# VectorE's maxima head by head around the copy of a turned head, and one scaling of the maxima, in a two-layer attention kernel on one core

## Chip, cores and metric

One core of one Trainium2 chip runs the whole kernel. The metric is the device time in microseconds, the median of the runs. TensorE is called PE in the profile, VectorE DVE, ScalarE ACT, GpSimd POOL; PEld is TensorE's loading of weights, which overlaps its products.

## The reference, cut to what matters

32 batches of x (112 rows of 256) and of a context (375 rows of 256) go through two layers. Each layer has a cross attention with 16 heads and a feed-forward part. What the change touches is the softmax of both attentions:

```python
# layer 0, 16 heads of width 64
sim = einsum('bihd,bjhd->bhij', q, k) * DIM_HEAD ** -0.5
attn = softmax(sim, axis=-1)              # over 375 positions
# layer 1, 16 heads of width 16, q and k normalised per head, then rotated
q = rms_norm(q, q_norm_w); k = rms_norm(k, k_norm_w)
attn = softmax(einsum('bhtd,bhsd->bhts', rope(q), rope(k)) * D ** -0.5, axis=-1)
```

The softmax subtracts the maximum of each row. In layer 1 the kernel multiplies q's normalising factor (one number for each row and head, in `qrs`) not into q, but into the exponential as its scale; so the negated maximum has to be multiplied by the same factor.

## The kernel before, in words

Everything of a batch lives on chip. Each engine runs its own instruction list, written out by hand, and they meet at semaphores. After an opening part (layer 0 of batch 0) each engine runs a loop of 31 batches: `rest(b)`, which finishes layer 0 and the first feed-forward part and already projects keys, values and queries of batch b+1, and `attention(MIDDLE, b)`; a closing part does layer 1 of the last batch, and the second feed-forward part of all batches follows.

The attention goes by pairs of heads. The MIDDLE part has 16 pairs, i = 0 to 15: pairs 0 to 3 and 12 to 15 are of layer 0 (of the next batch), pairs 4 to 11 of layer 1. At step i the engines do the following, in this order:

- TensorE: `scores(i+2)` (L409, two heads, into two of the four banks of `ps`), `turn(i-1)` (L419, three transposes for each head of the pair, into the two banks of `pt`), and at odd steps from 3 the products with the values, `values0` (L431) or `values1` (L446), for earlier pairs. At the last two steps come projections of keys and values.
- VectorE: `row_max(i+2)`, `row_sum(i+1)` (L1024, the reciprocal of the sums), `turned(i-1)` (L999, the copy of the odd head's transposes from `pt` into `probT`).
- ScalarE: its own `turned(i-1)` (L734, the copy of the even head), then `exps(i+2)` (L773, two exponentials, each with its sum read out by a second instruction).
- GpSimd: the product of pair i+1 with the reciprocals (L1442), and in the first steps four roots for `qrs`.

The waits that tie them together:

- `scores(j+2)` waits for `exped`, the exponentials of pair j, since `ps` holds two pairs.
- `row_max(j)` waits for `scores(j)` of both heads; `exps(j)` waits for `maxed`.
- `turned(i-1)` waits for `pT`, the turn of its head.
- the second head of `turn(i)` waits for `pT_odd`, VectorE's copy of the turn before; the first head for `pT_even`, ScalarE's.
- `row_sum(i+1)` waits for the exponentials of pair i+1.

For layer 1, `row_max` before is a reduction, a wait of VectorE on itself (`link`, a semaphore `dve_steps`), at even pairs a wait for GpSimd's root (`q1_rstd`), and two scalings (L1016), one for each head. `HEADS1` puts heads h and h+4 together as a pair.

Of the kernel before, what the change touches and what calls it, by code (L numbers as in the profile page):

```python
# [10 lines left out]
ALU = mybir.AluOpType  # L11
ACT = mybir.ActivationFunctionType
AX_X = mybir.AxisListType.X
# [8 lines left out]
U8_EPS = 1e-8  # L22


DVE_STEPS = 29
POOL_STEPS = 7


# [24 lines left out]
def xattn_ffn_kernel(nc, A, x3_dram, out):  # L53
    B, T, D = A["x"].shape
    S = A["ctx"].shape[1]
    INNER = A["wq0"].shape[1]
    F = A["f0w1T"].shape[1]
    H = 16
# [16 lines left out]
    PAIRS = H // 2  # L75
    HEADS1 = [8 * c + n for c in range(DC) for n in (0, 4, 2, 6, 1, 5, 3, 7)]

    with ExitStack() as ctx:
        def sb(name, shape, dt=F32):
            return ctx.enter_context(nc.sbuf_tensor(name, shape, dt))  # L80

        def sem(name):
            return ctx.enter_context(nc.semaphore(name))


        ps = ctx.enter_context(nc.psum_tensor("ps", [P, 4, 512], F32))
# [86 lines left out]
        qrs = sb("qrs", [T, 3, H])  # L173
# [3 lines left out]
        nmx = sb("nmx", [T, 2 * H])  # L177
# [7 lines left out]
        def flat(t, dt=F32):  # L185
# [24 lines left out]
            "const_in wk0_in wv0_in wkv1_in f0w1_in f0w2_in late_in w_hi w_lo ident_ready zeros_ready "  # L210
            "wsum_ready wsum_done w_quant f1w1_in f1w2_in "
            "x_in ctx_in cT_ready cT_hi cT_lo k0_ready k0_sb v0_ready v0_sb var0 rstd0 xn0_ready xT0_ready xT0_sb "
            "q0_ready q0_sb xbo_ready scores maxed exped recip normed pT pT_even pT_odd pv o_sb wo_ready x1_ready "
            "var1 rstd1 xq_ready diag_ready xqT_ready rb_ready xqT_sb rb_sb kv1_ready kv1_sb h_ready h_sb conv0 "
            "conv_ready tanh_ready y_ready yT_ready am_ready hr_ready hq_ready hqT_ready hqT_sb ffn_ready x2_ready "
# [5 lines left out]
        s = {n: sem(n) for n in names}  # L221
        block = ctx.enter_context(nc.Block())

        AHEAD = 2
# [5 lines left out]
        OPENING, MIDDLE, CLOSING = range(3)  # L230

        def pair_of(i, part):

            if part == OPENING:
                return 0, i
            if part == CLOSING:
                return 1, i
            if i < LEAD:
                return 0, i
            return (1, i - LEAD) if i < LEAD + PAIRS else (0, i - PAIRS)  # L240

        def at(i, part, b):

            return i if part == OPENING else b * G + (PAIRS + i)
# [718 lines left out]
        def _(dve):  # L963
            step = Steps(s["dve_steps"], DVE_STEPS)

            def link(ins):
                step.link(dve, ins)
# [28 lines left out]
            def turned(i, part, b):  # L996

                dve.wait_ge(s["pT"], 2 * at(i, part, b) + 2)
                dve.tensor_copy(probT[:, 2 * (i % 4) + 1, :, :],  # L999
                                pt[0:SK, 1, 0:KT * T].rearrange("p (k t) -> p k t", k=KT))\  # L1000
                    .then_inc(s["pT_odd"], 1)

            def row_max(i, part, b):

                layer, p = pair_of(i, part)
                g = layer * H + 2 * p
                dve.wait_ge(s["scores"], at(i + 1, part, b))
                top = dve.tensor_reduce(nmx[:, g:g + 2], ps[0:T, 2 * (i % 2):2 * (i % 2) + 2, 0:S], AX_X, ALU.max,  # L1008
                                        negate=True)
                if layer == 1:  # L1010
                    link(top)
                    if p % 2 == 0:
                        dve.wait_ge(s["q1_rstd"], b * 4 + (p // 2 + 1))
                    for n in range(2):
                        h = HEADS1[2 * p + n]
                        top = dve.tensor_scalar(nmx[:, g + n:g + n + 1], nmx[:, g + n:g + n + 1], qrs[:, 2, h:h + 1],  # L1016
                                                None, ALU.mult)
                top.then_inc(s["maxed"], 1)

            def row_sum(i, part, b):  # L1020
                layer, p = pair_of(i, part)
                g = layer * H + 2 * p
                dve.wait_ge(s["exped"], at(i + 1, part, b))
                dve.reciprocal(rinv[:, g:g + 2], rsum[:, g:g + 2]).then_inc(s["recip"], 1)  # L1024

            def query_masks(b):
                dve.wait_ge(s["q1T_ready"], b + 1)
                dve.tensor_tensor(q1[:, 0, :, :], pt[:, 0, 0:T].unsqueeze(1).to_broadcast([P, 4, T]),
                                  mask1[:].unsqueeze(2).to_broadcast([P, 4, T]), ALU.mult).then_inc(s["q1_sb"], 1)

            def query_squares(b):
                dve.wait_ge(s["q1_sq"], b + 1)
                link(dve.tensor_reduce(qrs[:, 0, :], qsq.rearrange("p (h e) -> p h e", e=DH1), AX_X, ALU.add))
                dve.tensor_scalar(qrs[:, 1, :], qrs[:, 0, :], 1.0 / DH1, RMS_EPS, ALU.mult, ALU.add)\
                    .then_inc(s["q1_var"], 1)
# [51 lines left out]
            def attention(part, b):  # L1087
                count = G if part == MIDDLE else PAIRS
                k = 0 if part == OPENING else b + 1
                for i in range(count):  # L1090
                    if part == OPENING and i in (2, 4, 6):
                        ternary(1, i // 2 + 1)
                    if i + AHEAD < count:
                        row_max(i + AHEAD, part, b)
                    if part == MIDDLE and i == 0:
                        query_masks(b)
                    if i + 1 < count:
                        row_sum(i + 1, part, b)
                    if part == MIDDLE and i == 0:
                        query_squares(b)  # L1100
                    if i >= 1:
                        turned(i - 1, part, b)
                if part != CLOSING:
                    k1_squares(k, 0)
                    k1_squares(k, 1)
                turned(count - 1, part, b)
                if part != CLOSING:
                    k1_squares(k, 2)
                    dve.wait_ge(s["k1_sq"], k * KT + KT)
                    dve.tensor_scalar(krs[:, 1, :], krs[:, 0, :], 1.0 / DH1, RMS_EPS, ALU.mult, ALU.add)\  # L1110
                        .then_inc(s["k1_var"], 1)
                if part == MIDDLE:
                    for n in range(5):
                        x3_step(n, b)
# [17 lines left out]
            def rest(b, last_batch):  # L1132
# [76 lines left out]
                if not last_batch:  # L1209
                    q0_copy(b + 1, 1)  # L1210
                    row_max(0, MIDDLE, b)
                else:
                    scales(1, 1)
# [10 lines left out]
                if not last_batch:  # L1224
                    row_sum(0, MIDDLE, b)
                    row_max(1, MIDDLE, b)
                else:
                    query_masks(b)
                    query_squares(b)
                    for i in range(AHEAD):  # L1230
                        row_max(i, CLOSING, b)
                    row_sum(0, CLOSING, b)


# [28 lines left out]
            for rope, w in ((ropq[:].unsqueeze(1), nwq), (ropk[:], nwk)):  # L1263
                n, k = rope.shape[0], rope.shape[1]
# [327 lines left out]
```

## Time and profile before

| | |
|---|---|
| median of 3 runs | 2452.87 us (2451.51 to 2453.61) |
| profiled execution, its own time | 2455.66 us |
| its span, first to last instruction | 2453.8 us |
| TensorE busy | 2380.4 us, 97% |
| VectorE, ScalarE, GpSimd busy | 1700.6, 1584.0, 1596.3 us (69, 65, 65%) |
| one batch of the loop | 70.93 us |
| mean granted TensorE clock | 0.985 |

The profile is of one execution, so its sums are compared with its own time. A busy share is an average over the span; the timeline and the chain of waits, read in one batch, show who waits for whom. Instructions on one engine overlap a little: one starts before the record of the one ahead ends.

### The profile page before, as it was taken

What the parts mean: (1) busy time and instruction counts of PE and PEld (TensorE: products, weight loads), DVE (VectorE), ACT (ScalarE), POOL (GpSimd) and SP (SyncE); (2) the same over time, 40 slices, a digit from 0 to 9 for tenths busy, and PEclk for the clock granted to TensorE, in tenths of its full rate; (3) what the DMA queues carried; (4) which work ended last, traced back from release to release, by engine and by line L of the source; (5) the groups of instructions that cost most, each with busy time, mean ns of one, the idle gap of its engine ahead of it and who ended that gap; (6) DMA issues with size and microseconds to landing.
All of it is one profiled execution on the core that took longest, in us unless ns stands there. A gap on an engine that the chain in (4) does not pass through costs nothing.

```text
span 2453.8 us, 59494 instructions
## 1 busy us (share of the span) xinstructions
PE 2380.4 (97%) x18926; PEld 1796.5 (73%) x18926; DVE 1700.6 (69%) x4476; ACT 1584.0 (65%) x4337; POOL 1596.3 (65%) x1862
## 2 busy tenths in 40 slices
PE   7999999999999999999999999999999999999578
PEld 5777777777777777777777777777777777777336
DVE  6666666776667667666767776666677666767775
ACT  4666666766666676666666766666676666667346
POOL 2666776666667666666776666677666666766507
PEclk9999999999999999999999999999999999999689
DMA  4100000000000000000000000000000000000202
GB/s 151 35 10 10 10 8 4 8 10 10 10 10 8 10 2 10 10 10 10 10 8 4 8 10 10 10 10 8 7 5 10 10 10 10 8 4 0 55 10 61
DMA packets 34652, 37.02 MB, mean 15 GB/s; under 512 B 2932, under 2 KB 33092, under 8 KB 34628
## 3 DMA queue, kind: packets, MB, share of 16 engines
q1 hardware_dynamic: 34628, 36.71, 5.0%
q8 instruction: 14, 0.23, 0.0%
q14 instruction: 10, 0.08, 0.0%
HBM read 29.36 MB, written 7.34 MB: 15 GB/s over the span
## 4 chain that ended last, share of the span: by engine, by line
PE 86%; ACT 5%; DVE 4%; issue 2%; POOL 1%; DMA 0%; ACTq 0%; POOLq 0%; DVEq 0%; SPq 0%
PE ps L334 24%; PE ps L409 15%; PE pt L419 14%; PE pa L431 5%; PE pa L466 5%; PE ps L393 5%; PE pa L446 4%; ACT prob L773 3%; PE pa L334 2%; PE pt L334 2%; PE pa L593 1%; PE pa L553 1%; DVE nmx L1008 1%; PE pt L577 1%; PE ps L459 1%
## 5 line engine op out<-in xcount | busy, mean ns | idle before, releaser
L1008 DVE TENSOR_REDUCE nmx<-ps 112x2 f32<-112x750 f32 x512 | 476.5, 936 | 203.4 <-PE ps L409 203.3
L1442 POOL TENSOR_TENSOR prob<-prob,rinv 112x375 f32<-112x375 f32 x512 | 404.0, 810 | 286.6 <-DVE rinv L1024 280.6
L1442 POOL TENSOR_TENSOR f1w_room<-f1w_room,rinv 112x375 f32<-112x375 f32 x512 | 404.6, 814 | 33.4 <-DVE rinv L1024 27.2
L734 ACT ACTIVATE room<-ps 128x375 f32<-128x375 f32 (+2 forms) x480 | 227.8, 488 | 278.3 <-PE ps L334 278.3
L999 DVE COPY probT<-pt 125x336 f32<-125x336 f32 x512 | 253.0, 494 | 98.8 <-PE pt L419 98.6
L734 ACT ACTIVATE probT<-pt 125x336 f32<-125x336 f32 x512 | 233.7, 456 | 107.8 <-PE pt L419 104.9
L419 PEld LDWEIGHTS pt<-ident,prob 112*125 112x125 f32 x1536 | 191.5, 189 | 130.3 <-issue 91.7
L419 PEld LDWEIGHTS pt<-ident,f1w_room 112*125 112x125 f32 x1536 | 197.8, 188 | 119.4 <-POOL f1w_room L1442 52.7
L1465 POOL TENSOR_TENSOR krs<-krs,nhalf 125x48 f32<-125x48 f32 x32 | 256.9, 8028 | 0.0
L419 PE MATMUL pt<-ident,f1w_room 112*125 112x112 f32 x1536 | 238.2, 287 | 2.8 <-DVE probT L999 1.2
L419 PE MATMUL pt<-ident,prob 112*125 112x112 f32 x1536 | 239.1, 291 | 0.0
L409 PE MATMUL ps<-kT,q 64*112 64x375 f32 x1024 | 231.3, 530 | 5.8 <-ACT prob L773 1.6
L409 PE MATMUL ps<-room,q 64*112 64x375 f32 x1024 | 220.5, 518 | 3.0 <-ACT prob L773 1.9
L773 ACT ACTIVATE prob<-ps,nmx 112x375 f32<-112x375 f32 x256 | 144.4, 569 | 84.8 <-DVE nmx L1008 83.2
L773 ACT ACTIVATE prob<-ps,nmx,qrs 112x375 f32<-112x375 f32 x256 | 169.0, 674 | 45.3 <-DVE nmx L1016 45.3
L773 ACT ACTIVATE f1w_room<-ps,nmx,qrs 112x375 f32<-112x375 f32 x256 | 168.3, 668 | 33.3 <-DVE nmx L1016 33.3
L431 PE MATMUL pa<-probT,room 125*64 125x112 f32 x3072 | 183.6, 265 | 0.0
L1429 POOL TENSOR_TENSOR st<-st,lneps 112x1 f32<-112x1 f32 x96 | 18.2, 190 | 252.6 <-DVE st L990 252.6
L431 PEld LDWEIGHTS pa<-probT,room 125*64 125x64 f32 x3072 | 149.2, 137 | 24.9 <-issue 11.0
L773 ACT ACTIVATE f1w_room<-ps,nmx 112x375 f32<-112x375 f32 x256 | 144.3, 571 | 4.6 <-DVE nmx L1008 1.4
L334 PE MATMUL ps<-cT_hi,wk_lo 128*128 128x376 f32 x512 | 138.2, 351 | 6.7 <-DVE cT_lo L972 6.7
L1169 DVE SCALAR_TENSOR_TENSOR z<-hp,convw,z 128x112 f32<-128x112 f32 x512 | 138.7, 330 | 3.5
(262 smaller groups left out, 5168.7 us busy)
## 6 DMA issues: line engine op xcount, KB each, us to landing
ctok<-in_ctx SPq DMA_DIRECT2D x32, 375.0 KB
xin<-in_x SPq DMA_DIRECT2D x32, 112.0 KB, 2.0
x_rows<-x SPq DMA_DIRECT2D x32, 112.0 KB, 1.9
out<-probT SPq DMA_DIRECT2D x16, 224.0 KB, 2.3
room<-x_rows SPq DMA_DIRECT2D x1, 2576.0 KB, 13.9
stage<-in_f1w SPq DMA_DIRECT2D x2, 1024.0 KB, 5.3
stage<-in_wk SPq DMA_DIRECT2D x1, 1024.0 KB, 8.0
stage<-in_wv SPq DMA_DIRECT2D x1, 1024.0 KB, 10.5
```

The source lines that it names most:

```text
L334: last = pe.matmul(dst, left(l, c), right(r, c), start=(n == 0), stop=(n == len(TERMS) - 1))
L393: last = pe.matmul(ps[:, g + 1, j * T:(j + 1) * T], wq0[:, c, (HT * g + j) * P:(HT * g + j + 1) * P], xn0T[:, c, :], start=(c == 0), stop= ...
L409: last = pe.matmul(ps[0:T, 2 * (i % 2) + n, 0:S], q, k, start=True, stop=True)
L419: last = pe.transpose(pt[0:SK, n, t * T:(t + 1) * T], prob(i, n)[:, t * SK:(t + 1) * SK], ident[0:T, 0:T])
L431: last = pe.matmul(pa[r:r + DH0, p // HT, (p % HT) * T:(p % HT + 1) * T], v0[0:SK, t, h * DH0:(h + 1) * DH0], probT[:, 2 * (i % 4) + n, t, :],
L734: return act.activation(dst, src, ACT.Copy)
L773: ins = act.activation(prob(i, n), ps[0:T, 2 * (i % 2) + n, 0:S], ACT.Exp, bias=nmx[:, g:g + 1], scale=scale, accum_out=rsum[:, g:g + 1])
L999: dve.tensor_copy(probT[:, 2 * (i % 4) + 1, :, :], pt[0:SK, 1, 0:KT * T].rearrange("p (k t) -> p k t", k=KT))\
L1008: top = dve.tensor_reduce(nmx[:, g:g + 2], ps[0:T, 2 * (i % 2):2 * (i % 2) + 2, 0:S], AX_X, ALU.max, negate=True)
L1169: ins = dve.scalar_tensor_tensor(z[:, j, :], hp[:, j, tap:tap + T], convw[:, j, tap:tap + 1], z[:, j, :], ALU.mult, ALU.add)
L1442: pool.tensor_tensor(prob(i, n), prob(i, n), rinv[:, g:g + 1].to_broadcast([T, S]), ALU.mult).then_inc(s["normed"], 1)
L1465: step.link(pool, pool.tensor_tensor(krs[:, 2, :], krs[:, 1, :], nhalf[0:SK, :], ALU.pow))
```

## The change

In every even step from 2 on that still has a pair i+2 to come, VectorE takes the maximum of the first head of pair i+2, then copies the odd turned head of pair i-1, then takes the maximum of the second head. In the other steps the maximum is taken over both heads at once, as before, and the copy stays last. The scaling of the maxima in layer 1 leaves `row_max`: it becomes `max_scale`, one tensor-tensor operation for both heads, which stands behind `row_sum(i+1)` and waits for a new semaphore `top1` that the last reduction raises, in place of VectorE's wait on itself (so a batch has 21 of these linked steps and not 29).

```diff
-DVE_STEPS = 29
+DVE_STEPS = 21
@@
-            def row_max(i, part, b):
+            def row_max(i, part, b, heads=slice(0, 2)):
 
                 layer, p = pair_of(i, part)
-                g = layer * H + 2 * p
+                g, m = layer * H + 2 * p, 2 * (i % 2)
                 dve.wait_ge(s["scores"], at(i + 1, part, b))
-                top = dve.tensor_reduce(nmx[:, g:g + 2], ps[0:T, 2 * (i % 2):2 * (i % 2) + 2, 0:S], AX_X, ALU.max,
-                                        negate=True)
+                top = dve.tensor_reduce(nmx[:, g + heads.start:g + heads.stop],
+                                        ps[0:T, m + heads.start:m + heads.stop, 0:S], AX_X, ALU.max, negate=True)
+                if heads.stop == 2 and layer == 0:
+                    top.then_inc(s["maxed"], 1)
+                elif heads.stop == 2:
+                    top.then_inc(s["top1"], 1)
+
+            def max_scale(i, part, b):
+                layer, p = pair_of(i, part)
                 if layer == 1:
-                    link(top)
+                    g, h = H + 2 * p, HEADS1[2 * p]
+                    assert HEADS1[2 * p + 1] == h + 4
+                    dve.wait_ge(s["top1"], b * PAIRS + (p + 1))
                     if p % 2 == 0:
                         dve.wait_ge(s["q1_rstd"], b * 4 + (p // 2 + 1))
-                    for n in range(2):
-                        h = HEADS1[2 * p + n]
-                        top = dve.tensor_scalar(nmx[:, g + n:g + n + 1], nmx[:, g + n:g + n + 1], qrs[:, 2, h:h + 1],
-                                                None, ALU.mult)
-                top.then_inc(s["maxed"], 1)
+                    dve.tensor_tensor(nmx[:, g:g + 2], nmx[:, g:g + 2], qrs[:, 2, h:h + 5:4], ALU.mult)\
+                        .then_inc(s["maxed"], 1)
@@ in attention, for each i
-                    if i + AHEAD < count:
+                    between = i >= 2 and i % 2 == 0 and i + AHEAD < count
+                    if between:
+                        row_max(i + AHEAD, part, b, slice(0, 1))
+                        turned(i - 1, part, b)
+                        row_max(i + AHEAD, part, b, slice(1, 2))
+                    elif i + AHEAD < count:
                         row_max(i + AHEAD, part, b)
                     if part == MIDDLE and i == 0:
                         query_masks(b)
                     if i + 1 < count:
                         row_sum(i + 1, part, b)
+                    if i + AHEAD < count:
+                        max_scale(i + AHEAD, part, b)
                     if part == MIDDLE and i == 0:
                         query_squares(b)
-                    if i >= 1:
+                    if i >= 1 and not between:
                         turned(i - 1, part, b)
@@ in rest, last batch
                     for i in range(AHEAD):
                         row_max(i, CLOSING, b)
+                        max_scale(i, CLOSING, b)
```

## Rows read from the trace of the kernel before

**Rows 1.** The page: busy us, share of the span, instructions of each engine.

```profile
PE 2380.4 (97%) x18926; PEld 1796.5 (73%) x18926; DVE 1700.6 (69%) x4476; ACT 1584.0 (65%) x4337; POOL 1596.3 (65%) x1862
```

**Rows 2.** Windows, one batch: length, each engine's busy time, granted clock, DMA.

```profile
1023.73:1094.66 70.93, 70.78 (x573) 53.84 (x574) 49.44 (x135) 47.08 (x132) 48.16 (x58) 1.00 0.03 9
```

**Rows 3.** Timeline of steps 8 and 9: start, length, engine, line, idle time before.

```profile
1040.93 0.89 PE L409 MATMUL ps<-kT,q 64*112 64x375 f32 x4
...
1041.75 0.91 PE L419 MATMUL pt<-ident,f1w_room 112*125 112x112 f32 x6
1041.87 0.94 DVE L1008 TENSOR_REDUCE nmx<-ps 112x2 f32<-112x750 f32 x1 [0.54 <-PE ps L409]
...
1042.93 0.33 DVE L1016 TENSOR_SCALAR nmx<-nmx,qrs 112x1 f32<-112x1 f32 x2
...
1043.26 0.49 DVE L999 COPY probT<-pt 125x336 f32<-125x336 f32 x1
...
1043.40 1.03 PE L419 MATMUL pt<-ident,prob 112*125 112x112 f32 x6
...
1043.43 0.67 ACT L773 ACTIVATE f1w_room<-ps,nmx,qrs 112x375 f32<-112x375 f32 x1 [0.62 <-DVE nmx L1016]
1043.66 0.93 DVE L1008 TENSOR_REDUCE nmx<-ps 112x2 f32<-112x750 f32 x1
...
1044.64 0.20 ACT L773 ACTIVATION_READ_ACCUMULATOR f1w_room<-ps,nmx,qrs 112x1 f32 x1
...
1045.08 0.89 PE L409 MATMUL ps<-room,q 64*112 64x375 f32 x4
```

**Rows 4.** Chain that ended last, steps 2 to 5: start, length, what.

```profile
1028.07 0.95 DVE nmx L1008
...
1029.25 0.35 DVE nmx L1016 x2
...
1033.52 0.26 ACT prob L773
...
1033.82 0.89 PE ps L409 x4
```

**Rows 5.** Timeline of TensorE alone, steps 3 to 6.

```profile
1029.60 1.16 PE L419 MATMUL pt<-ident,f1w_room 112*125 112x112 f32 x6
...
1032.81 0.91 PE L419 MATMUL pt<-ident,f1w_room 112*125 112x112 f32 x6
...
1036.78 0.57 PE L409 MATMUL ps<-kT,q 64*112 64x375 f32 x2
```

**Rows 6.** VectorE's groups by form: out<-in, count, busy us, mean ns, idle.

```profile
L1184 DVE TENSOR_REDUCE am<-pa 112x1 f32<-112x512 f32 x64 | 43.9, 686 | 4.2 <-PE pa L553 0.5
...
L1039 DVE TENSOR_REDUCE krs<-room 125x16 f32<-125x256 f32 x96 | 39.9, 416 | 111.9 <-ACT v L734 111.9
...
L972 DVE TENSOR_TENSOR cT_lo<-ps,cT_hi 128x375 fp32r<-128x375 f32 x64 | 32.1, 544 | 18.3 <-ACT cT_hi L734 18.3
...
L1322 DVE TENSOR_TENSOR t<-t 128x2 f32<-128x2 f32 x1 | 0.2, 161 | 0.0
```

**Rows 7.** Timeline of steps 12 to 14.

```profile
1049.10 0.89 PE L409 MATMUL ps<-room,q 64*112 64x375 f32 x4
...
1050.04 0.94 DVE L1008 TENSOR_REDUCE nmx<-ps 112x2 f32<-112x750 f32 x1 [0.95 <-PE ps L409]
...
1051.01 0.57 ACT L773 ACTIVATE f1w_room<-ps,nmx 112x375 f32<-112x375 f32 x1
...
1052.03 0.20 ACT L773 ACTIVATION_READ_ACCUMULATOR f1w_room<-ps,nmx 112x1 f32 x1
...
1052.19 0.45 ACT L734 ACTIVATE probT<-pt 125x336 f32<-125x336 f32 x1
...
1053.12 0.58 PE L419 MATMUL pt<-ident,prob 112*125 112x112 f32 x3
```

**Rows 8.** Windows, 40 us behind the loop, in the closing part.

```profile
2280.00:2320.00 40.00, 22.28 (x92) 14.14 (x94) 28.39 (x73) 15.75 (x42) 23.91 (x16) 0.50 0.16 39
```

More of the change, by code:

```diff
@@ L212, in xattn_ffn_kernel @@
             "x_in ctx_in cT_ready cT_hi cT_lo k0_ready k0_sb v0_ready v0_sb var0 rstd0 xn0_ready xT0_ready xT0_sb "
-            "q0_ready q0_sb xbo_ready scores maxed exped recip normed pT pT_even pT_odd pv o_sb wo_ready x1_ready "
+            "q0_ready q0_sb xbo_ready scores top1 maxed exped recip normed pT pT_even pT_odd pv o_sb wo_ready x1_ready "
             "var1 rstd1 xq_ready diag_ready xqT_ready rb_ready xqT_sb rb_sb kv1_ready kv1_sb h_ready h_sb conv0 "
```

## The prediction

> **What bounds the kernel now.** I read the profile from coarse to fine. The page's busy line first: TensorE is busy 97% of the span, the other three engines 65 to 69% [rows 1]. The windows of one batch say it more sharply: a batch of the steady loop takes 70.93 us and TensorE works in 70.78 us of them [rows 2]; 31 such batches are 2199 us, nine tenths of the span. The granted clock there is 1.00, the level of 2.4 GHz. So nothing that only frees VectorE (49.44 us of 70.93) can gain; the change matters where VectorE stands between two pieces of TensorE's work, in the attention.
>
> There one loop sets the pace. PSUM holds the scores of two pairs of heads, so scores(j+2) waits until ScalarE has taken the exponentials of pair j, these wait for the maxima of pair j (VectorE, "maxed"), and these wait for scores(j). Read it off for j = 10 in the timeline [rows 3], S being the start of scores(10), 1040.93. The reduction starts at 1041.87 (S+0.94) and takes 0.94; the two scalings start 0.12 after its end, at 1042.93, and take 0.33; ScalarE starts 0.17 later, at 1043.43, and its last piece ends at 1044.84, 1.41 later; TensorE starts 0.05 behind such an end (1033.78 to 1033.82 in the chain of waits [rows 4]). Sum: 0.94+0.94+0.12+0.33+0.17+1.41+0.05 = 3.96 us. TensorE comes to scores(12) at 1045.08, S+4.15. **The loop has 0.19 us of slack**, and no more.
>
> TensorE's 4.15 is not all work. The turn in step 8 (1041.75) lasts 0.91, that in step 9 (1043.40) lasts 1.03 [rows 3]: its second head waits for VectorE's copy of the turn before, which ends only at 1043.75, since VectorE has first taken the maxima and their scaling. That 0.12 recurs in step 7. In step 3 the same wait makes the turn 1.16 long, 0.25 too much [rows 5]. And scores(7) waits for ScalarE until 1033.82 [rows 4], where the turn in front, begun at 1032.81 [rows 5], ends at 1033.72 and would have given way 0.07 earlier, as scores(10) does to its turn (1041.75 against 1041.82 [rows 3]): at 1033.65, so 0.17 are lost. All that VectorE's order costs TensorE: 0.12+0.12+0.25+0.17 = 0.66 us a batch.
>
> **The change, part by part.** In the even steps 2, 4, ..., 12 (pairs 4, 6, ..., 14) the reduction over 112x750 becomes two over 112x375, with the copy of the turned odd head between them.
>
> *The copy.* It can't start before the turn of that step has ended, and TensorE does that turn behind the scores: it ends at 1041.75+0.91 = 1042.66, S+1.73. With the 0.05 that VectorE shows behind TensorE (1041.82 to 1041.87) the copy starts at S+1.78 where it started at S+2.33. It comes 0.55 earlier and takes away the three turn waits: at most 0.49 us a batch.
>
> *The second head's maximum.* It now stands behind that copy. Head 0 needs S+0.94 to S+1.49 and then VectorE idles 0.29 us for the turn. Copy to S+2.27 (0.49). The next instruction starts 0.09 before a copy's end (1043.75 against 1043.66 [rows 3]): S+2.18. Its length isn't in the trace. The nearest rows: 256 elements 416 ns, 512 elements 686 ns, and an operation over 375 elements out of PSUM 544 ns [rows 6]. Reductions thus cost about 1.05 ns an element and 150 ns for themselves; I take 0.55 us, with 0.42 and 0.69 as ends. End at S+2.73, where the whole maximum ended at S+1.88.
>
> The Trainium skill says that such a fixed cost is paid by every instruction, so that many small tiles pay it often (VectorE: DVE Perf Modes, "The TRN2 errata"); the rows above agree. Its table gives a Vector operation out of PSUM 120 cycles and one for each element, at 0.96 GHz 516 ns for 375, an estimate from that page; by it the loss below would be some 5 us smaller in all.
>
> *The scaling (layer 1).* One tensor-tensor operation over 112x2 for two tensor-scalars. A tensor-tensor over 128x2 takes 161 ns [rows 6], two scalings 0.33: 0.17 saved. The wait for the root of the same step stays, so does the 0.12 in front. Start S+2.85, end S+3.01. Ends: 0.15 and 0.21 (one of today's scalings, 0.33 for two that overlap by 0.08).
>
> *The order.* The scaling also moves behind the row sum's reciprocal, which waits for the exponentials of pair i+1. In odd steps these end about when they are needed: the maxima of pair j+1 then reach ScalarE about 0.2 us late. In even steps the row sum comes about 0.5 us later for GpSimd, which works 48.16 us of 70.93 [rows 2] and has its result needed a step later. I cost both at nothing, because the loop over the even pairs, below, is longer than either; were it not, the first would cost up to 0.19 in each of four steps.
>
> **The new loop:** 3.01 + 0.17 + 1.41 + 0.05 = **4.64 us** for layer 1, against 4.15 now and 4.03 of pure TensorE work. Without a scaling and with the shorter exponentials of layer 0 (1051.01 to 1052.23, 1.22 [rows 7]) and with ScalarE 0.03 behind a maximum (1050.98 to 1051.01 [rows 7]; no root is waited for) it is 2.73 + 0.03 + 1.22 + 0.05 = 4.03, against 4.02.
>
> Along one batch:
> - Pair 4. Maximum in front at 1028.07, so S = 1027.13. Here 0.23 lie between reduction and scaling (1029.02 to 1029.25 [rows 4]). New end of scaling: S+2.73+0.23+0.16 = 1030.25, against 1029.60: 0.65 late. From there to scores(7) the chain is ScalarE alone without a wait [rows 4], so scores(7) comes 0.65 later. That swallows the 0.25 and the 0.17.
> - Pair 6: scores(8) comes 2.96 behind scores(7) (1036.78 against 1033.82 [rows 4, 5]), and its loop, begun at scores(6), ends earlier: nothing added.
> - Pairs 8 and 10: 4.64 for 4.15, twice 0.49. The 0.12 of each is inside.
> - Pair 12: 4.03 for 4.02: 0.01.
> - Pair 14: nothing waits for its scores, but the turn of pair 13 needs ScalarE's even copy of pair 12, which is queued behind the exponentials of pair 14. These end at S+2.73+0.03+1.22 = S+3.98; the copy takes 0.45, overlapping by 0.04 (1052.19 against 1052.23), and I give TensorE 0.1 behind a copy, twice what it shows behind an exponential, for the stretched turn of 1043.40 ends 0.68 behind its copy: S+4.49. Today it starts at 1053.12, S+4.02 [rows 7]: 0.47.
>
> Sum: 0.65+0.49+0.49+0.01+0.47 = 2.11, say **2.1 us a batch**. Nothing later in the batch gives it back, since TensorE has no idle time there. 31 x 2.1 = 65.1. The opening and the closing part have two such steps each; partly at half clock, where TensorE's own work hides more, I take 0.8 together. The profiled execution took 2455.66 (span 2453.80, 1.86 outside it), so 2521.6 for it; the median of the runs lies 2.8 lower: **2519 us**, 2.7% slower. With the ends for the half maximum (0.13 either way, in four or five places) the batch loses 1.6 to 2.8 us: 2503 to 2540.
>
> **Rivals.**
> - *The copy frees TensorE (faster).* If the second head's maximum did not lie on the loop, 0.66 us a batch would come back: 20 us, 2433. It decides at a loop of 4.03 us: the half maximum and the scaling would have to end 0.6 us earlier than I find, yet the copy can't precede the turn, which ends at S+1.73. 3 in 100. That loss and gain just meet (2453): 2 in 100.
> - *Only the steady pairs pay.* ScalarE might start pair 4 later without passing it on, and the even copy of pair 12 might slip in earlier; then 2 x 0.49 remain, 31 us: 2484. Against it speaks that ScalarE runs strictly in order in [rows 4]. 12 in 100.
> - *The odd steps pay too.* The scaling behind the row sum adds 0.19 in four steps: 24 us more, 2543. For it: the wait is real. Against it: it runs beside the longer loop. 7 in 100.
> - *The clock falls.* Late in the span, where TensorE works 22.28 of 40 us, the granted clock is 0.50, its level of 1.2 GHz [rows 8]. The new loop still works 4.03 of 4.64 us, and 0.6 us is the longest hole. If it did fall in the attention, 4.03 would be 8.06 a pair of steps, 3.4 more, eight times a batch: over 800 us. The Trainium skill has the clock fall after idle time (TensorE: Matmul & The Clock Gate, "The HAM clock gate"); whether it does after holes this short no row shows. 2 in 100.
>
> My case keeps 74 in 100, with a range of its own of 2503 to 2540. The range for 8 in 10 reaches some way towards the case where only the steady pairs pay and stops at my own upper end: 2492 to 2540. About 0.2% (5 us) is what a measurement of this kernel can tell from no change: faster 0.03, same 0.02, slower 0.95.
>
> **What would show it.** In the new trace a batch takes 73.0 us, and most of the 2.1 more is TensorE idle; scores(8), (10), (12) start 4.64 apart; idle time of the weight loads in front of the scores is put down to ScalarE's exponentials, and ScalarE's to VectorE's scaling; half maxima take 0.55, one waits 0.3 for TensorE's turn between them; turns are 0.91 long, none stretched. I am wrong if the steps 8 to 11 still take 4.15 a pair, if the half maximum is far from 0.55, or if the turn, not the scores, is what waits.

## The result, and the profile after

The changed kernel takes 2516.27 us (median of 4 runs, 2514.64 to 2519.22); the kernel before takes 2452.19 beside it (2450.04 to 2453.61). The ratio is 1.0262 [1.0248, 1.0276]: 64 us slower, where 66 (2519 us) was predicted. The profiled execution took 2515.62 us, its span is 2513.8, its mean granted clock 0.987.

The page's busy line, its chain of waits in shares, and the windows of one batch, as [rows 1] and [rows 2]:

```profile
PE 2373.5 (94%) x18926; PEld 1783.7 (71%) x18926; DVE 1704.7 (68%) x4410; ACT 1571.9 (63%) x4337; POOL 1593.9 (63%) x1862
...
PE 54%; POOL 27%; issue 13%; DVE 5%; ACT 1%; DMA 0%; POOLq 0%; SPq 0%; ACTq 0%; DVEq 0%
```

```profile
1048.40:1121.37 72.97, 70.70 (x574) 53.53 (x573) 49.59 (x133) 46.70 (x132) 48.09 (x58) 1.00 0.03 8
```

A batch takes 72.97 us, 2.04 more than in [rows 2], with the same work in it (70.70 busy against 70.78) at the same clock. All of the loss is TensorE waiting, 2.27 us a batch where it was 0.15. (A turn that is stretched by a wait counts as busy for its whole length, so busy time is a little more than work.) 31 x 2.04 = 63 us.

Where it waits: steps 8 and 9 from the timeline, beside [rows 3] (S, the start of scores(10), is 1066.70).

```profile
1066.70 0.89 PE L409 MATMUL ps<-kT,q 64*112 64x375 f32 x4 [0.54 <-ACT prob L773]
...
1067.52 0.91 PE L419 MATMUL pt<-ident,f1w_room 112*125 112x112 f32 x6
...
1067.64 0.55 DVE L1008 TENSOR_REDUCE nmx<-ps 112x1 f32<-112x375 f32 x1 [0.32 <-PE ps L409]
...
1068.46 0.51 DVE L999 COPY probT<-pt 125x336 f32<-125x336 f32 x1 [0.28 <-PE pt L419]
1068.89 0.54 DVE L1008 TENSOR_REDUCE nmx<-ps 112x1 f32<-112x375 f32 x1
...
1069.21 0.91 PE L419 MATMUL pt<-ident,prob 112*125 112x112 f32 x6
...
1069.55 0.16 DVE L1023 TENSOR_TENSOR nmx<-nmx,qrs 112x2 f32<-112x2 f32 x1
...
1069.88 0.67 ACT L773 ACTIVATE f1w_room<-ps,nmx,qrs 112x375 f32<-112x375 f32 x1 [1.20 <-PE pt L419]
...
1071.08 0.20 ACT L773 ACTIVATION_READ_ACCUMULATOR f1w_room<-ps,nmx,qrs 112x1 f32 x1
...
1071.34 0.57 PE L409 MATMUL ps<-room,q 64*112 64x375 f32 x2 [0.51 <-ACT f1w_room L773]
```

The first half maximum ends at S+1.49, VectorE idles 0.28 until the turn has ended, the copy starts at S+1.76, the second half at S+2.19, the scaling at S+2.85, ScalarE at S+3.18, and the next scores at S+4.64. Where the rows of before had 0.12 stretches in the turns, both turns here are 0.91 long.

Two labels mislead. ScalarE's wait at 1069.88 is put down to a turn of TensorE; but ScalarE starts 0.17 behind the scaling's end (1069.71), as in [rows 3], and in the experiments the loop grows by just what the scaling grows. And the chain of waits runs through GpSimd, 27% of the span:

```profile
1066.92 1.58 POOL prob L1456 x2
1068.51 1.04 issue
...
1069.58 1.58 POOL prob L1456 x2
```

Between its products lie "issue" gaps, 1.04 us here and up to 1.31 in this batch. In them GpSimd waits for VectorE's reciprocal of the row sums, which stands behind the late second half: an effect, unless GpSimd's product is what TensorE waits for. An experiment below asks that.

### The profile page after: what moved, and what is told of

Its sections match the earlier page's. It is cut to its first block, busy times and chain, and to the rows that moved or that the text cites. A ratio compares the mean times of both kernels' runs of the same rounds, so it can differ in the third digit from the quotient of the medians.

```text
span 2513.8 us, 59180 instructions
## 1 busy us (share of the span) xinstructions
PE 2373.5 (94%) x18926; PEld 1783.7 (71%) x18926; DVE 1704.7 (68%) x4410; ACT 1571.9 (63%) x4337; POOL 1593.9 (63%) x1862
## 4 chain that ended last, share of the span: by engine, by line
PE 54%; POOL 27%; issue 13%; DVE 5%; ACT 1%; DMA 0%; POOLq 0%; SPq 0%; ACTq 0%; DVEq 0%
PE ps L334 23%; POOL prob L1456 13%; POOL f1w_room L1456 11%; PE pa L466 5%; PE ps L393 5%; PE pa L431 3%; PE pt L419 3%; PE ps L409 3%; POOL qrs L1499 2%; PE pt L334 2%; PE pa L593 1%; PE pa L553 1%; DVE nmx L1008 1%; PE pt L577 1%; PE ps L459 1%
## 5 line engine op out<-in xcount | busy, mean ns | idle before, releaser
L1008 DVE TENSOR_REDUCE nmx<-ps 112x2 f32<-112x750 f32 x702 | 503.7, 722 | 96.9 <-PE ps L409 96.5
L419 PEld LDWEIGHTS pt<-ident,f1w_room 112*125 112x125 f32 x1536 | 189.5, 188 | 133.8 <-POOL f1w_room L1456 69.0
L419 PE MATMUL pt<-ident,prob 112*125 112x112 f32 x1536 | 234.0, 289 | 12.2 <-POOL prob L1456 11.5
L419 PE MATMUL pt<-ident,f1w_room 112*125 112x112 f32 x1536 | 227.2, 284 | 18.5 <-ACT probT L734 16.9
L1030 DVE RECIPROCAL rinv<-rsum 112x2 f32<-112x2 f32 x512 | 82.6, 161 | 142.1 <-ACT f1w_room L773 83.5
```

Source lines behind the costliest of these rows:

```text
L419: last = pe.transpose(pt[0:SK, n, t * T:(t + 1) * T], prob(i, n)[:, t * SK:(t + 1) * SK], ident[0:T, 0:T])
L1008: top = dve.tensor_reduce(nmx[:, g + heads.start:g + heads.stop], ps[0:T, m + heads.start:m + heads.stop, 0:S], AX_X, ALU.max, negate=True)
```

## The experiments

Each edit is made to the changed kernel. "Two scalings" stands for this edit of `max_scale`, the two operations of the kernel before in place of the one:

```diff
-                    dve.tensor_tensor(nmx[:, g:g + 2], nmx[:, g:g + 2], qrs[:, 2, h:h + 5:4], ALU.mult)\
-                        .then_inc(s["maxed"], 1)
+                    for n in range(2):
+                        h = HEADS1[2 * p + n]
+                        top = dve.tensor_scalar(nmx[:, g + n:g + n + 1], nmx[:, g + n:g + n + 1], qrs[:, 2, h:h + 1],
+                                                None, ALU.mult)
+                    top.then_inc(s["maxed"], 1)
```

All are read by the starts of TensorE's scores in one batch near the middle of the loop, in us:

| kernel | batch | scores 4 to 7 | 7 to 8 | 8 to 10 | 10 to 12 | 12 to 14 | median us | ratio |
|---|---|---|---|---|---|---|---|---|
| before | 70.93 | 6.69 | 2.96 | 4.15 | 4.15 | 4.02 | 2452.2 | 1 |
| after | 72.97 | 7.25 | 2.96 | 4.63 | 4.64 | 4.06 | 2516.3 | 1.0262 |
| scale_only | 71.07 | 6.92 | 3.13 | 4.02 | 4.02 | 4.02 | 2455.9 | 1.0024 [1.0014, 1.0034] |
| split_only | 71.08 | 6.92 | 3.12 | 4.03 | 4.03 | 4.02 | 2453.1 | 1.0011 [1.0001, 1.0020] |
| order_only | 73.48 | 7.43 | 2.96 | 4.81 | 4.81 | 4.03 | 2532.8 | 1.0337 [1.0320, 1.0354] |
| sum_in_hole | 73.97 | 7.25 | 2.95 | 5.13 | 5.12 | 4.06 | 2545.3 | 1.0392 [1.0375, 1.0409] |
| two_behind | 70.87 | 6.69 | 2.95 | 4.09 | 4.11 | 4.08 | 2450.3 | 0.9997 [0.9988, 1.0007] |
| hole_two | 74.24 | 7.43 | 3.13 | 5.00 | 4.99 | 4.24 | 2556.7 | 1.0438 [1.0422, 1.0455] |
| head_two | 70.72 | 6.42 | 3.13 | 4.02 | 4.02 | 4.03 | 2442.9 | 0.9968 [0.9956, 0.9980] |
| once_two | 70.73 | 6.61 | 2.96 | 4.08 | 4.09 | 4.02 | 2445.8 | 0.9981 [0.9972, 0.9991] |
| order_2 | 71.66 | 7.43 | 2.95 | 4.15 | 4.15 | 4.03 | 2474.1 | 1.0100 [1.0083, 1.0117] |
| order_6_8 | 72.13 | 6.61 | 2.96 | 4.80 | 4.81 | 4.02 | 2489.3 | 1.0158 [1.0141, 1.0175] |
| order_12 | 71.33 | 6.61 | 2.96 | 4.15 | 4.15 | 4.02 | 2464.7 | 1.0061 [1.0044, 1.0078] |
| hole_at_once | 73.64 | 7.43 | 3.13 | 4.81 | 4.81 | 4.03 | 2535.8 | 1.0349 [1.0331, 1.0366] |

The ratio of each is to runs of the kernel before beside it, whose medians were 2451.0 us for the first four experiments and 2449.5 and 2450.3 for the next two groups of four.

### Which part of the change costs the time

**scale_only**: no copy between; the whole maximum, the one scaling still behind the row sum.

```diff
-                    between = i >= 2 and i % 2 == 0 and i + AHEAD < count
+                    between = False
```

> Only the scaling is changed (one operation, behind the row sum); the maxima stay whole and the copy last. Theory (the loss is the loop through the late second maximum): with that maximum back in front, the loop is 0.17 us shorter than in the kernel before, the copy ends 0.25 earlier, and the four small waits of TensorE (0.66 us a batch) go: a batch of 70.27 us, about 2432 us. Rival 'the scaling behind the row sum's wait costs the time': slower than 2452, near 2500. Rival 'split or order costs nothing, GpSimd's late row sum is the bound': here the row sum comes no later than before, so 2452 or a little less.

**split_only**: two half maxima without the copy between them.

```diff
                         row_max(i + AHEAD, part, b, slice(0, 1))
-                        turned(i - 1, part, b)
                         row_max(i + AHEAD, part, b, slice(1, 2))
@@
-                    if i >= 1 and not between:
+                    if i >= 1:
                         turned(i - 1, part, b)
```

> The two half maxima stand back to back, the copy is last again; the rest as in the changed kernel. Theory: a half maximum costs 0.07 us beyond its share, less than the single scaling saves; the loop ends 0.1 earlier than in the kernel before: a batch near 70.3, about 2433 us. Rival 'two instructions in place of one are what costs': stays near 2516, or at least above 2452.

**order_only**: the new order, two scalings, directly behind the maxima.

```diff
                         row_max(i + AHEAD, part, b, slice(1, 2))
+                        max_scale(i + AHEAD, part, b)
                     elif i + AHEAD < count:
                         row_max(i + AHEAD, part, b)
+                        max_scale(i + AHEAD, part, b)
@@
-                    if i + AHEAD < count:
-                        max_scale(i + AHEAD, part, b)
```

> The maxima head by head with the copy between them, but the two old scalings, and they stand directly behind the second maximum, ahead of the row sum. Theory: the loop of pairs 4, 8 and 10 grows by the 0.17 that the single scaling saved, to 4.8 us: a batch 0.5 longer than the changed kernel's 72.97, about 2532 us. Rival 'the scaling behind the row sum costs the time': near 2452. Rival 'GpSimd is the bound': the row sum comes later still by 0.17 at each of these pairs, so it says the same as the theory here, about 2530.

Splitting costs nothing: scale_only and split_only have the same batch. Putting only the copy between the halves takes split_only's 2453.1 to the 2516.3 of after: **63 us for where the copy stands**. order_only came where it was expected; its loops are 4.81, which is 4.64 and the 0.17 by which two scalings (0.33) are longer than one (0.16).

But scale_only and split_only were expected some 20 us below before and aren't. Their even loops did fall to 4.02 and give back 2 x 0.13; scores 4 to 7 and 7 to 8 grew by 0.23 and 0.17. The timeline of scale_only, step 3, where it is plainest, and its group of scalings by form:

```profile
957.87 1.58 POOL L1456 TENSOR_TENSOR f1w_room<-f1w_room,rinv 112x375 f32<-112x375 f32 x2
...
958.64 0.82 DVE L1023 TENSOR_TENSOR nmx<-nmx,qrs 112x2 f32<-112x2 f32 x1
...
959.38 0.49 DVE L999 COPY probT<-pt 125x336 f32<-125x336 f32 x1
```

```profile
L1023 DVE TENSOR_TENSOR nmx<-nmx,qrs 112x2 f32<-112x2 f32 x256 | 109.9, 429 | 8.9 <-issue 5.3 <-DVE nmx L1008 0.4
```

An operation on 112x2 numbers takes 0.82 us: it ends at 959.46, GpSimd's product at 959.45. The mean is 429 ns, against 161 undisturbed. That is a second mechanism, which the prediction did not have: the one-piece scaling waits for GpSimd's product where it starts inside one, and the copy waits behind it.

What made the two stretches grow is this wait in the even steps 2 and 4, the scalings of pairs 4 and 6:

```profile
955.35 1.58 POOL L1456 TENSOR_TENSOR f1w_room<-f1w_room,rinv 112x375 f32<-112x375 f32 x2
...
956.39 0.56 DVE L1023 TENSOR_TENSOR nmx<-nmx,qrs 112x2 f32<-112x2 f32 x1 [0.17 <-issue]
...
957.12 0.66 ACT L773 ACTIVATE prob<-ps,nmx,qrs 112x375 f32<-112x375 f32 x1 [0.97 <-DVE nmx L1023]
```

```profile
960.38 1.58 POOL L1456 TENSOR_TENSOR prob<-prob,rinv 112x375 f32<-112x375 f32 x2
...
961.29 0.68 DVE L1023 TENSOR_TENSOR nmx<-nmx,qrs 112x2 f32<-112x2 f32 x1
...
962.01 1.08 PE L419 MATMUL pt<-ident,prob 112*125 112x112 f32 x6
```

In step 2 ScalarE starts pair 4 at 957.12, 2.85 behind scores(4) (954.27), where it was 2.63 in before. From there to scores(7) ScalarE has work without a break, so scores(7) comes 0.23 later. In step 4 the copy stands behind a scaling of 0.68, and the turn of step 5 waits for that copy: it is 1.08 long and not 0.91, the 0.17 from 7 to 8. The 0.82 of step 3 costs nothing, since ScalarE is not yet there.

**two_behind** tests that: `between = False` as in scale_only, and two scalings, at the same place.

> As scale_only (whole maxima, copy last, scaling behind the row sum), but the scaling is again two tensor-scalar operations. In scale_only the single tensor-tensor took up to 0.83 us where GpSimd was in a product, and ended 0.02 us behind it each time. Theory 'VectorE's operation with two inputs in SBUF waits for GpSimd's instruction': no scaling over 0.25 us here, the copy 0.07 us earlier than in the kernel before, about 2447 us (2443 to 2452). Rival 'it is the place behind the row sum that costs': 2456 or more, with long waits in front of the scaling.

```profile
L1025 DVE TENSOR_SCALAR nmx<-nmx,qrs 112x1 f32<-112x1 f32 x512 | 83.1, 204 | 9.1 <-issue 5.7
```

At the same place, beside the same products, the two scalings take 204 ns each, and both grown stretches are back (6.69, 2.95). So the form of the operation, not its place, makes the wait. (That every long scaling ends with a product says what it waits for.)

### Is GpSimd the bound of the new kernel?

**sum_in_hole**: the row sum moves into the hole in front of the copy, so that GpSimd gets its reciprocals earlier.

```diff
                         row_max(i + AHEAD, part, b, slice(0, 1))
+                        row_sum(i + 1, part, b)
                         turned(i - 1, part, b)
@@
-                    if i + 1 < count:
+                    if i + 1 < count and not between:
                         row_sum(i + 1, part, b)
```

> As the changed kernel, but in the even steps the row sum stands between the first half maximum and the copy, in the 0.3 us in which VectorE waits for TensorE's turn. GpSimd then gets it about 0.9 us earlier, and nothing on the loop moves. Theory: no change against the changed kernel, 2514 to 2519 us. Rival 'GpSimd, 27% of the chain after, is the bound because its row sum comes late': 10 to 60 us faster, 2456 to 2506.

**hole_two**: the same with two scalings, at the place of after's. **hole_at_once**: the same with two scalings placed as in order_only, directly behind the maxima.

> As sum_in_hole (maxima head by head, row sum in front of the copy), but two tensor-scalar scalings. Theory 'tensor-tensor waits for GpSimd': sum_in_hole was slower than the changed kernel only because the early row sum set GpSimd to work while VectorE scaled; two short scalings cost 0.17 on the loop and no wait: scores(8), (10) and (12) start 4.80 apart (5.13 in sum_in_hole), about 2530 us, below sum_in_hole's 2545. Rival 'the early row sum delays the copy or the second maximum': 2545 + 0.5 a batch, about 2560.

> order_only with the row sum of the even steps moved in front of the copy. In sum_in_hole and hole_two the scaling of the odd steps stood behind a row sum as well, so that both row sums, each waiting for ScalarE's exponentials, lay on one chain. Theory: with the scaling directly behind the maximum the odd pair's exponentials end in time, the early row sum costs nothing, a batch takes order_only's 73.48 us, about 2533 us. Rival 'an early row sum delays the copy by itself': 2545 to 2560.

sum_in_hole gave neither answer: its loops are 5.13. Step 8 of its timeline:

```profile
1001.41 2.50 POOL L1457 TENSOR_TENSOR f1w_room<-f1w_room,rinv 112x375 f32<-112x375 f32 x3
...
1002.62 0.54 DVE L1008 TENSOR_REDUCE nmx<-ps 112x1 f32<-112x375 f32 x1
...
1003.28 0.65 DVE L1023 TENSOR_TENSOR nmx<-nmx,qrs 112x2 f32<-112x2 f32 x1
...
1004.10 0.66 ACT L773 ACTIVATE prob<-ps,nmx,qrs 112x375 f32<-112x375 f32 x1 [1.70 <-DVE nmx L1023]
```

GpSimd started earlier, and its product now lies over the scaling of the even step: the scaling ends 0.02 behind it (1003.93 against 1003.91) and takes 0.65 instead of 0.16, 0.49 on the loop, 4.64 + 0.49 = 5.13.

hole_two takes that wait away and should have had loops of 4.81; it has 5.00, a miss. Its timeline in an even step:

```profile
1003.70 0.91 PE L419 MATMUL pt<-ident,prob 112*125 112x112 f32 x6
...
1004.72 0.17 DVE L1033 RECIPROCAL rinv<-rsum 112x2 f32<-112x2 f32 x1 [0.36 <-ACT f1w_room L773]
...
1004.83 0.51 DVE L999 COPY probT<-pt 125x336 f32<-125x336 f32 x1
1005.25 0.54 DVE L1008 TENSOR_REDUCE nmx<-ps 112x1 f32<-112x375 f32 x1
```

The copy could have started 0.05 behind the turn's end (1004.61), at 1004.66, and starts at 1004.83: the reciprocal in front of it waits for ScalarE. ScalarE is late since in odd steps the scaling stands behind a row sum that itself waits for exponentials, so that exponentials, row sum, scaling and the next exponentials form one series. If so, taking the odd steps' scaling out from behind the row sum must bring 4.81 back. hole_at_once does so: 4.81, batch 73.64 against order_only's 73.48, 2536 us where 2533 was expected. Its GpSimd gets the reciprocals in front of the copy and nothing is gained; 0.17 are even lost from 7 to 8, where TensorE waits for ScalarE. So in order_only, whose loops are after's with a longer scaling, **GpSimd is not the bound**, although its chain of waits runs through GpSimd as that of after does. For after itself this is carried over, not tested alone: sum_in_hole was to do that, and its scaling wait hid the answer.

### Which steps pay

order_only with the new order in some even steps alone, in the loop alone: **order_2** (pair 4), **order_6_8** (pairs 8 and 10), **order_12** (pair 14).

```diff
-                    between = i >= 2 and i % 2 == 0 and i + AHEAD < count
+                    between = part == MIDDLE and i == 2
```

(`i in (6, 8)` and `i == 12` in the others.)

> The kernel before with the maxima head by head around the copy in step 2 of each batch alone (pair 4); two scalings directly behind the maximum everywhere. Theory: scores(7) comes 0.74 us later through ScalarE's queue, as in order_only, and nothing gives it back; the two turn waits of steps 7 and 9 stay. A batch of 71.67 us, about 2474 us. Rival 'ScalarE makes up for a late start of pair 4': 2452 to 2460.

> The same in steps 6 and 8 alone (pairs 8 and 10). Theory: scores(8) to (10) and (10) to (12) take 4.81 us each for 4.15: 1.32 a batch, 72.25 us, about 2492 us.

> The same in step 12 alone (pair 14, layer 0). Theory: nothing waits for this pair's scores, but the turn of pair 13 needs ScalarE's copy of pair 12, queued behind the late exponentials: 0.45 a batch, 71.4 us, about 2466 us. Rival 'the last pair is free, as its scores hold nobody up': 2452. The three kernels' extra times should add up to that of order_only (2533).

All three came within 3 us. They stand 23.9, 39.0 and 14.4 us above their before (2450.3), together 77.3, where order_only is 81.9 above its own: the steps add up, nearly. The missing part is in the table: where pair 4 keeps its whole maximum (order_6_8, order_12), scores 4 to 7 take 6.61 and not 6.69, though these kernels change nothing in step 2 but the semaphore between maximum and scaling. The scaling of pair 4 starts 0.13 behind its reduction there, in the timeline of before 0.25 (0.23 in its chain of waits). Twice 0.08 in 31 batches are 5.0 us. Pair 4 pays, and pair 14 too. Of the latter the table shows nothing, since its 0.48 lies behind scores(14) (from there to the query turn of the next batch 45.49 us in before, 45.96 in after, 45.97 in order_12). It is in front of turn(13), in after:

```profile
1079.27 0.44 ACT L734 ACTIVATE probT<-pt 125x336 f32<-125x336 f32 x1
...
1079.86 0.88 PE L419 MATMUL pt<-ident,prob 112*125 112x112 f32 x6 [0.37 <-POOL prob L1456]
```

The page names GpSimd as the releaser; the prediction named ScalarE's copy. In hole_at_once GpSimd had its reciprocals earlier, yet the turn came as late, 4.46 us behind scores(14) in both:

```profile
1011.77 2.35 POOL L1460 TENSOR_TENSOR prob<-prob,rinv 112x375 f32<-112x375 f32 x3
...
1014.64 0.45 ACT L734 ACTIVATE probT<-pt 125x336 f32<-125x336 f32 x1
...
1015.23 0.88 PE L419 MATMUL pt<-ident,prob 112*125 112x112 f32 x6 [0.37 <-ACT probT L734]
```

The turn starts 0.14 behind the copy's end here (1015.09) and 0.15 in after (1079.71), while GpSimd's product ended 1.11 before it here (1014.12) and 0.02 before it in after (1079.84). It follows the copy.

### What of the idea is of use

**once_two**: the copy behind the whole maximum and the two scalings, but in front of the row sum (except in the first and last steps), the halves given up. **head_two**: the new order, with the maxima handed to ScalarE head by head, so that the first head's exponential doesn't wait for the second head's maximum; the semaphores `maxed` and `top1` count heads and not pairs, and each head has its own tensor-scalar scaling. Both diffs are cut to what matters: the calls of `max_scale` and `turned` that stood behind the row sum go away, and the other steps scale directly behind their maximum.

```diff
@@ once_two, in attention
                         row_max(i + AHEAD, part, b)
+                        max_scale(i + AHEAD, part, b)
+                    if i >= 2 and i + AHEAD < count:
+                        turned(i - 1, part, b)
                     if i + 1 < count:
                         row_sum(i + 1, part, b)
```

```diff
@@ head_two, exps
-                act.wait_ge(s["maxed"], at(i + 1, part, b))
                 for n in range(2):
+                    act.wait_ge(s["maxed"], 2 * at(i, part, b) + n + 1)
@@ head_two, in attention
                         row_max(i + AHEAD, part, b, slice(0, 1))
+                        max_scale(i + AHEAD, part, b, slice(0, 1))
                         turned(i - 1, part, b)
                         row_max(i + AHEAD, part, b, slice(1, 2))
+                        max_scale(i + AHEAD, part, b, slice(1, 2))
```

> Whole maxima, the two old scalings directly behind them, and the copy ahead of the row sum (from step 2 on): only the row sum and the copy of the kernel before are exchanged. Theory: the copy comes 0.07 us earlier, which takes 0.07 off each of three turn waits and leaves the loop alone: 0.2 us a batch, about 2446 us (0.27% faster). Rival 'the later row sum hurts through GpSimd': no faster than 2452.

> As the changed kernel, but ScalarE is released for each head by itself: the first head's maximum is scaled in the hole in front of the copy, the exponential of the first head starts then, and behind the copy only the second head's maximum, its scaling and one exponential follow; scalings are tensor-scalars, directly behind the maxima. Theory (loop through the late second maximum): the loop falls from 4.64 to about 4.03 us, as long as TensorE's own work; the copy is early and no turn waits: a batch 70.3 to 70.5, about 2433 us, faster than both. Rival 'the split or the early copy itself costs': not below 2452.

once_two came out at its number, in part by luck. Of its 0.2 us a batch, 0.07 and 0.06 are the two turn waits of steps 7 and 9, as forecast. The 0.08 from scores 4 to 7 are not the copy's: order_6_8 and order_12, whose copy stays last in step 2, have them too. Its expectation calls it the kernel before with only the row sum and the copy exchanged; the wait in front of the scaling is another too.

head_two beats both kernels, 0.32% [0.20, 0.44] below before, though by less than expected. Step 8 of its timeline, step 5, and the windows of one batch:

```profile
960.83 0.55 DVE L1008 TENSOR_REDUCE nmx<-ps 112x1 f32<-112x375 f32 x1 [1.16 <-PE ps L409]
...
961.50 0.21 DVE L1022 TENSOR_SCALAR nmx<-nmx,qrs 112x1 f32<-112x1 f32 x1
...
961.66 0.51 DVE L999 COPY probT<-pt 125x336 f32<-125x336 f32 x1
961.75 0.66 ACT L773 ACTIVATE prob<-ps,nmx,qrs 112x375 f32<-112x375 f32 x1
962.08 0.54 DVE L1008 TENSOR_REDUCE nmx<-ps 112x1 f32<-112x375 f32 x1
...
962.66 0.21 DVE L1022 TENSOR_SCALAR nmx<-nmx,qrs 112x1 f32<-112x1 f32 x1
...
962.90 0.67 ACT L773 ACTIVATE prob<-ps,nmx,qrs 112x375 f32<-112x375 f32 x1 [0.40 <-DVE nmx L1022]
```

```profile
956.45 1.59 POOL L1456 TENSOR_TENSOR prob<-prob,rinv 112x375 f32<-112x375 f32 x2
...
957.58 1.08 PE L419 MATMUL pt<-ident,prob 112*125 112x112 f32 x6
```

```profile
946.88:1017.60 70.72, 70.62 (x575) 53.75 (x573) 50.08 (x141) 47.10 (x132) 48.06 (x58) 1.00 0.03 9
```

ScalarE starts the first head 0.04 behind its scaling, beside the copy; the second head's maximum still comes late (0.40 idle), but only one exponential hangs on it. The loop is 4.02, all TensorE's work, 0.13 less than before in two places. Scores 4 to 7 gain 0.27; 0.17 is lost again from 7 to 8 and 0.14 behind scores(14): 0.21 a batch, 6.5 us of the 6.6 measured. The two losses are why it missed 2433, and here GpSimd is the one waited for: its product of step 5 ends at 958.04, the second head of the turn starts 0.05 behind such an end, and the turn is 1.08 long instead of 0.91; behind scores(14) it is nearly the same, 1.07. That the busy time is 70.62 of 70.72 us doesn't show that nothing is left, since these stretches are in it: some 0.3 us a batch are, an estimate from the two, and no run here takes them back.

## Why the prediction was right, point by point

- **The loop decides.** Right, and shown: every time in it matches to 0.02 us, and taking the copy out from between the halves alone takes the loss away (split_only). The rule "the copy can't precede the turn, and the second head stands behind the copy" is the cause.
- **The half maximum**, 0.55 with ends 0.42 and 0.69: right. All 380, beside the 112x750 form and the scaling:

```profile
L1008 DVE TENSOR_REDUCE nmx<-ps 112x2 f32<-112x750 f32 x322 | 297.8, 933 | 42.2 <-PE ps L409 41.9
...
L1008 DVE TENSOR_REDUCE nmx<-ps 112x1 f32<-112x375 f32 x380 | 206.6, 544 | 54.7 <-PE ps L409 54.7
...
L1023 DVE TENSOR_TENSOR nmx<-nmx,qrs 112x2 f32<-112x2 f32 x256 | 55.1, 215 | 6.6
```

  2 x 544 - 933 = 155 ns is what an instruction costs for itself. The 516 ns from the page's table (Trainium skill, VectorE: DVE Perf Modes, "The TRN2 errata") is 28 ns too low here; the trace decides. What that section says of many small tiles it says of operations that read SBUF. These read PSUM, and that the cost is paid by each of them is what the 155 ns show.
- **The terms of the sum.** Pairs 8 and 10: 0.48 and 0.49 for 0.49 each. Pair 14: 0.44 and 0.03 behind it for 0.47. Pair 12: 0.04 for 0.01. Pair 4: 0.56 for 0.65. Together 2.04 for 2.11. The mis-sized term is pair 4: the 0.23 between its reduction and its scaling was taken over from before, and it is 0.13 now (1054.59 to 1054.72, below). That isn't because the scaling comes later: order_6_8 and order_12, with the new semaphore and the scaling at its old time, have 0.13 as well, and two_behind, with the row sum in front, has 0.25. What the rest of the 0.23 was stays open.
- **"I cost both at nothing."** Right in the sum, for a reason that was only half seen. The even steps hid the reordering of the odd ones, as argued. The odd steps' scaling, however, did not take the 0.16 assumed:

```profile
1054.05 0.54 DVE L1008 TENSOR_REDUCE nmx<-ps 112x1 f32<-112x375 f32 x1
...
1054.72 0.16 DVE L1023 TENSOR_TENSOR nmx<-nmx,qrs 112x2 f32<-112x2 f32 x1
...
1055.46 1.58 POOL L1456 TENSOR_TENSOR f1w_room<-f1w_room,rinv 112x375 f32<-112x375 f32 x2
...
1056.57 0.49 DVE L1023 TENSOR_TENSOR nmx<-nmx,qrs 112x2 f32<-112x2 f32 x1
```

  It takes 0.49 in step 3, ending 0.02 behind GpSimd's product (1057.04). It cost nothing because ScalarE had other work first and took up pair 5 only at 1057.62, 0.56 after the scaling's end. In the even steps the 0.16 was right, but for pairs 4 and 6 only because the late second maximum puts the scaling behind GpSimd's products. With the maximum early again it falls into them: 0.23 and 0.17 a batch in scale_only. The prediction had no term for that.
- **The rivals.** That only the steady pairs pay is refuted (order_2, order_12), and so is, for the change itself, that the odd steps pay too: its even loops are 4.64, and a series through the odd steps showed only in hole_two (5.00). The clock stayed at 1.00 in the loop. The freed copy does give TensorE the 0.12 stretches back, but only where the loop is below 4.15 (scale_only, head_two).
- **What was to be shown.** Batch 73.0: 72.97. Scores(8), (10) and (12) 4.64 apart: 4.63 and 4.64. The weight loads in front of the scores wait for ScalarE's exponentials: yes, 0.78 us in front of scores(10). ScalarE's wait labelled with VectorE's scaling: no, the label names TensorE's turn.
- Outside the loop the predicted 0.8 us for opening and closing part can't be told apart: those parts differ by more than that, in the other direction, between the two profiled executions (63 us in the loop, 60.0 between the spans).

## What to carry to other kernels

Before an operation is put between two halves of another, ask what the inserted one waits for: here a copy that can't start before S+1.78 was put in front of half of a maximum that was due at S+1.88, on a loop with 0.19 us of slack. Finishing work by halves pays only if the consumer takes it by halves too; with that hand-over the order was 0.3% faster than the kernel before, without it (order_only) 3.4% slower. (How much of this 0.3% is the earlier scaling of pair 4, worth 0.08 us a batch or 0.1% in order_6_8 and order_12, was not tested.) And an edit that costs nothing beside a longer loop has been sized only for that loop: here the merged scaling took 0.16 us in steps 2 and 4 of the changed kernel, and 0.56 and 0.68 as soon as the copy no longer stood in front of it.

## What the runs showed of the hardware that was not expected

The VectorE tensor-tensor operation over 112x2, with both inputs in SBUF, waits until GpSimd's running product ends, and then ends 0.01 to 0.02 us behind it: 0.82, 0.65 and 0.49 us for numbers that otherwise take 0.16. In scale_only 125 of 256 did, and the mean was 429 ns. As two tensor-scalar operations over 112x1, which take the factor as a scalar for each row, the same arithmetic beside the same products took 204 ns each and never waited in this way. The Trainium skill says so (SBUF — State Buffer, "Who interferes with whom"): a VectorE instruction with two SBUF inputs contends with a GpSimd instruction that reads SBUF, whoever issues first holds the shared port pair for its whole instruction, and one with at most one SBUF input doesn't contend outside the 2-port perf modes. The traces agree for the products.

Two things limit the rule of thumb. One SBUF input is no protection by itself. In before, the tensor-scalar over 112x16 with two constants starts inside a product in 31 of 32 batches; it takes 0.57 us there and ends 0.03 behind the product, against 0.18 in the one batch without:

```profile
1025.70 1.57 POOL L1442 TENSOR_TENSOR prob<-prob,rinv 112x375 f32<-112x375 f32 x2 [1.67 <-DVE rinv L1024]
...
1025.97 0.57 DVE L1034 TENSOR_SCALAR qrs<-qrs 112x16 f32<-112x16 f32 x1
```

And not every operation of GpSimd holds VectorE up. Its roots read SBUF too and last 1.01 us, but 63 scalings of after ran beside one in 0.15 to 0.16 us; there the traces don't agree with the Trainium skill's rule as it stands. No run here tests either point by itself.

Merging two small operations into one can so lengthen them; the saving of 0.17 that was predicted holds only in the steps in which no product of GpSimd runs.
